# Attention loop: softmax division in place in PSUM, output projection in three rounded passes, mask product in one pass, side jobs in other rounds

## The reference, cut to what matters

```python
q = (x @ Wq).reshape(b, s, 16, 64)          # b = 1, s = 2048, x is [2048, 128]
k = (x @ Wk).reshape(b, s, 16, 64)
v = (x @ Wv).reshape(b, s, 16, 64)
dot = jnp.einsum('bihd,bkhd->bhik', q, k)
w = jax.nn.softmax(dot / jnp.sqrt(64.), axis=-1)
a = jnp.einsum('bhij,bjhd->bihd', w, v).reshape(b, s, 1024)
out = a @ Wo + bo
```

## Time and profile before

| | us |
|---|---|
| median of 3 runs (1913.63 to 1916.16) | 1915.83 |
| the profiled execution | 1917.79 |
| its span, first to last instruction | 1916.5 |
| TensorE busy | 1685.4 (88%) |
| VectorE busy | 1327.3 (69%) |
| GpSimd busy | 1286.8 (67%) |
| ScalarE busy | 787.4 (41%) |
| 32 maximum-and-score units, about 443 to 1739 | some 1300 |

### The profile page before, as it was taken

The page is one execution under the profiler, slowest core; times in us unless marked ns, Lnnn a source line. Parts: engine busy times, 40 slices in busy tenths (PEclk is TensorE's granted clock), DMA queues, the critical chain, the costliest instruction groups (busy, mean ns, idle before and its releaser), DMA issues.

```text
span 1916.5 us, 34532 instructions
## 1 busy us (share of the span) xinstructions
PE 1685.4 (88%) x13785; PEld 986.1 (51%) x13785; DVE 1327.3 (69%) x2083; ACT 787.4 (41%) x1183; POOL 1286.8 (67%) x652
## 2 busy tenths in 40 slices
PE   4988851848999999999999999999999999995793
PEld 3766641825555555555555555555555545442483
DVE  3566545666777777777777777777777788764575
ACT  3455430523444444444444444444444444442221
POOL 2233303135988888888888888888888889894303
PEclk8677755969999999999999999999999999997797
DMA  7000000210000000000000000000000000002112
GB/s 237 3 3 3 4 1 20 62 28 1 1 1 1 1 1 1 1 1 1 1 1 1 1 1 1 1 1 1 1 1 1 1 1 1 1 1 81 49 42 61
DMA packets 35190, 29.70 MB, mean 15 GB/s; under 512 B 4060, under 2 KB 30928, under 8 KB 35032
## 3 DMA queue, kind: packets, MB, share of 16 engines
q1 hardware_dynamic: 27064, 20.28, 3.5%
q0 software_dynamic: 2048, 4.20, 0.7%
q10 hardware_dynamic: 5920, 3.01, 0.5%
HBM read 18.31 MB, written 9.18 MB: 14 GB/s over the span
## 4 chain that ended last, share of the span: by engine, by line
PE 68%; DVE 8%; issue 6%; POOL 3%; DMA 1%; ACT 1%; DVEq 0%; POOLq 0%
PE psum L1799 22%; PE psum L1784 16%; PE psum L1759 9%; PE psum L1781 6%; DVE a_On L1994 3%; DVE a_mx L1962 3%; PE psum L1431 2%; PE psum L1813 2%; PE psum L1807 2%; PE psum L1732 1%; PE psum L1392 1%; PE psum L1207 1%; PE psum L1219 1%; PE psum L1441 1%; PE psum L1733 1%
## 5 line engine op out<-in xcount | busy, mean ns | idle before, releaser
L2075 POOL TENSOR_TENSOR a_acc<-a_acc,a_Pb 128x1024 f32<-128x1024 f32 x448 | 1066.0, 2379 | 147.0 <-ACT a_Pb L1899 102.0
L1962 DVE TENSOR_REDUCE a_mx<-psum 128x2 f32<-128x1024 f32 x512 | 624.9, 1223 | 274.7 <-PE psum L1759 274.2
L1899 ACT ACTIVATE a_Pb<-psum 128x1024 f32<-128x1024 f32 x512 | 498.1, 1024 | 646.5 <-PE psum L1784 646.5
L1799 PE MATMUL psum<-a_Pb,a_Vb 128*64 128x512 f32 x2048 | 494.1, 603 | 0.0
L1799 PEld LDWEIGHTS psum<-a_Pb,a_Vb 128*64 128x64 f32 x2048 | 127.0, 136 | 242.5 <-issue 171.8
L1759 PE MATMUL psum<-a_Kh,a_Qh 64*128 64x512 f32 x1024 | 237.3, 457 | 15.5 <-DVE a_mx L1962 15.0
L1759 PEld LDWEIGHTS psum<-a_Kh,a_Qh 64*128 64x128 f32 x1024 | 99.2, 184 | 251.9 <-issue 243.2
L1781 PE MATMUL psum<-a_Mr,a_ones_r 64*128 64x512 f32 x1024 | 203.8, 393 | 0.0
L1784 PE MATMUL psum<-a_Qh,a_Kh 64*128 64x512 f32 x1024 | 202.9, 391 | 0.0
L1784 PE MATMUL psum<-a_Ql,a_Kh 64*128 64x512 f32 x1024 | 202.8, 391 | 0.0
L1784 PE MATMUL psum<-a_Qh,a_Kl 64*128 64x512 f32 x1024 | 202.3, 389 | 0.0
(11 more groups left out here) (372 smaller groups left out, 1905.1 us busy)
## 6 DMA issues: line engine op xcount, KB each, us to landing
x_rows<-zero ACTq DMA_DIRECT2D x2, 1472.0 KB, 15.7
g_w<-in_L_ffn_w_eDF_dram SPq DMA_DIRECT2D x2, 1408.0 KB, 8.8
r_W<-in_L_ffn_W_dram SPq DMA_DIRECT2D x1, 2048.0 KB, 11.5
r_tile_x<-x_rows SPq DMA_DIRECT2D x23, 64.0 KB, 1.9
y_rows<-r_tile_y SPq DMA_DIRECT2D x23, 64.0 KB, 1.5
g_tile_x<-x_rows SPq DMA_DIRECT2D x23, 64.0 KB, 1.9
y_rows<-g_tile_y SPq DMA_DIRECT2D x23, 64.0 KB, 1.5
g_w<-in_L_ffn_w_eFD_dram SPq DMA_DIRECT2D x2, 512.0 KB, 10.8
```

Of the source, the lines that this page charges most:

```text
L1799: last = pe.matmul(ps[HEAD[h], B_O, :], b.Vb[:, p // 2 % 2, kc, at], b.Pb[:, step % BUFS, h * QT:(h + 1) * QT], start=(kc == 0), stop=(kc ...
L1899: act.activation(b.Pb[:, step % BUFS, :], ps[:, slot:slot + 2, :].rearrange("p a b -> p (a b)"), ACT.Exp, scale=SCALE).then_inc(S["probs"], 1)
L1962: v.tensor_reduce(b.mx[:, :, qc, quarter:quarter + 1], ps[:, bank:bank + 2, :], AX.X, ALU.max).then_inc(S[f"free{bank}"], 1)
L2075: g.tensor_tensor(b.acc[:, u, :], before, b.Pb[:, step % BUFS, :], ALU.add).then_inc(S["added"], 1)
```

## The change

What it does:

- The sums stay in bank 7. VectorE inverts them there, in four parts of 128 columns, two in round 2 and two in round 3. It multiplies them by `Or` in one instruction of 512 columns, in the same bank, at the end of round 3.
- ScalarE copies the result, rounded, into `Onh`; VectorE subtracts this in round 4 into `Onl`, which frees bank 7. `ssum`, `rec` and `On` go.
- `Wo` is split into a high and a low part at the start, as the three other weights are, and the output projection becomes three rounded passes, in round 5 of the next unit.
- `mask` multiplies two float32r operands; a rounded identity is made for it.
- `out` moves from round 2 (for unit U - 2) to round 5 (for unit U - 1), `v` from round 3 to round 6.

```diff
@@ misc_job
-    if d == 2 and U > 1:
-        return "out", U - 2
...
+    if d == 5 and U:
+        return "out", U - 1
...
@@ attention_weights_act, attention_weights_pool: four matrices where there were three
-    k.nc.scalar.wait_ge(k.S["att_w"], 48)
-    for m in range(3):
-        k.nc.scalar.activation(k.att_w[m][0][:, :], k.att_raw[:, m, :], ACT.Copy).then_inc(k.S["w_high"], 1)
+    k.nc.scalar.wait_ge(k.S["att_w"], 64)
+    for m, (hi, _) in enumerate((*k.att_w, k.att_o)):
+        k.nc.scalar.activation(hi[:, :], k.att_raw[:, m, :], ACT.Copy).then_inc(k.S["w_high"], 1)
...
@@ attention_pe
     def mask(U):
+        if U == 0:
+            pe.wait_ge(S["ident_r"], 1)
         pe.wait_ge(S["negated"], U + 1)
         bank = begin(("mask", U))
-        end(pe.matmul(ps[:, bank, 0:P], b.nm[:, :], k.ident[:, :], start=True, stop=True), bank)
+        end(pe.matmul(ps[:, bank, 0:P], b.nm[:, :], b.ident[:, :], start=True, stop=True), bank)
...
     def output(U):
-        pe.wait_ge(S["normalised"], 4 * U + 4)
+        freed(("sum", U))
         bank = begin(("out", U))
-        end(pe.matmul(ps[:, bank, :], k.att_o[:, U // NU, :], b.On[:, :], start=True, stop=True), bank)
+        hi, lo = (w[:, U // NU * P:(U // NU + 1) * P] for w in k.att_o)
+        pe.matmul(ps[:, bank, :], hi, b.Onh[:, :], start=True, stop=False)
+        pe.matmul(ps[:, bank, :], lo, b.Onh[:, :], start=False, stop=False)
+        end(pe.matmul(ps[:, bank, :], hi, b.Onl[:, :], start=False, stop=True), bank)
@@ attention_act
-    def sums(U):
-        bank = begin(("sum", U))
+    def normalised(U):
+        act.wait_ge(S["normalised"], U + 1)
         if U:
-            act.wait_ge(S["inverted"], 4 * U)
-        act.activation(b.ssum[:, :], ps[:, bank, :], ACT.Copy).then_inc(S[f"free{bank}"], 1)
+            bank, n = plan.at["out", U - 1]
+            act.wait_ge(S[f"full{bank}"], n)
+        act.activation(b.Onh[:, :], ps[:, plan.at["sum", U][0], :], ACT.Copy).then_inc(S["high_out"], 1)
...
-        if key and key[0] == "sum":
-            sums(U - 1)
         if d == 0 and U:
             heads_out(U - 1)
+        if d == 3 and U:
+            normalised(U - 1)
@@ attention_dve
     def invert(U, part):
-        if U and part == 0:
-            v.wait_ge(S["normalised"], 4 * U)
-        bank, n = plan.at["sum", U]
-        v.wait_ge(S[f"free{bank}"], n)
+        bank = begin(("sum", U))
         at = slice(part * P, (part + 1) * P)
-        v.reciprocal(b.rec[:, at], b.ssum[:, at]).then_inc(S["inverted"], 1)
+        v.reciprocal(ps[:, bank, at], ps[:, bank, at]).then_inc(S["inverted"], 1)
+
+    def normalise(U):
+        v.wait_ge(S["inverted"], 4 * U + 4)
+        v.wait_ge(S["heads_out"], U + 1)
+        bank = plan.at["sum", U][0]
+        v.tensor_tensor(ps[:, bank, :], ps[:, bank, :], b.Or[:, U % 2, :], ALU.mult).then_inc(S["normalised"], 1)
+
+    def normalised_low(U):
+        bank = plan.at["sum", U][0]
+        v.wait_ge(S["high_out"], U + 1)
+        if U:
+            last_out, n = plan.at["out", U - 1]
+            v.wait_ge(S[f"full{last_out}"], n)
+        v.tensor_tensor(b.Onl[:, :], ps[:, bank, :], b.Onh[:, :].bitcast(F32), ALU.subtract).then_inc(S[f"free{bank}"], 1)
...
-        if U and 2 <= d <= 5:
-            invert(U - 1, d - 2)
+        if U and d in (2, 3):
+            for part in (2 * d - 4, 2 * d - 3):
+                invert(U - 1, part)
+        if U and d == 4:
+            normalised_low(U - 1)
...
-        if U and d in (3, 5, 6, 7):
-            normalise(U - 1, (3, 5, 6, 7).index(d))
+        if U and d == 3:
+            normalise(U - 1)
```

More of the change, by code:

```diff
@@ L1594, in misc_job @@
         return "sum", U - 1
-    if d == 2 and U > 1:
-        return "out", U - 2
-    if d == 3 and p // 2 < PAIRS // 2 - 1:
-        return "v", p // 2 + 1, U % RN
     if d == 4 and U < UNITS - 2:
         return "q", U + 2
+    if d == 5 and U:
+        return "out", U - 1
+    if d == 6 and p // 2 < PAIRS // 2 - 1:
+        return "v", p // 2 + 1, U % RN
     if d == 7 and U < UNITS - 1:
@@ L1638, in __init__ @@
                 self.job(misc_job(R), B_P)
-        for key in (("out", UNITS - 2), ("sum", UNITS - 1), ("out", UNITS - 1)):
+        for key in (("sum", UNITS - 1), ("out", UNITS - 1)):
             self.job(key, B_P)
@@ L1656, in allocate_attention_weights @@
     k.att_w = [[k.sb(f"att_W{a}{part}", [P, PAIRS * P], F32R) for part in "hl"] for a in "qkv"]
-    k.att_o, k.att_b = k.sb("att_Wo", [P, PAIRS, P]), k.sb("att_b", [P, 1])
+    k.att_o = [k.sb(f"att_Wo{part}", [P, PAIRS * P], F32R) for part in "hl"]
+    k.att_b = k.sb("att_b", [P, 1])
 def allocate_attention_raw(k, mem):
-    k.att_raw = k.sb("att_raw", [P, 3, PAIRS * P], F32, mem)
+    k.att_raw = k.sb("att_raw", [P, 4, PAIRS * P], F32, mem)
 def allocate_attention(k, mem):
@@ L1676, in allocate_attention @@
     b.Or = sb("Or", [P, 2, QT])
-    b.On = sb("On", [P, QT])
-    b.ssum = sb("ssum", [P, QT])
-    b.rec = sb("rec", [P, QT])
+    b.Onh, b.Onl = (sb(a, [P, QT], F32R) for a in ("Onh", "Onl"))
     b.mx = sb("mx", [P, 2, 4, NU])
-    b.nm = sb("nm", [P, P])
+    b.nm = sb("nm", [P, P], F32R)
+    b.ident = sb("ident_r", [P, P], F32R)
     b.plan = Plan()
@@ L1688, in attention_loads_sp @@
         sp.dma_start(k.att_raw[:, m, :], io[name]).then_inc(S["att_w"], 16)
-    sp.dma_start(k.att_o[:, :, :], io["L1_attn_Wo"].rearrange("(a p) d -> p a d", p=P)).then_inc(S["att_wo"], 16)
+    sp.dma_start(k.att_raw[:, 3, :].rearrange("p (a d) -> p a d", a=PAIRS), io["L1_attn_Wo"].rearrange("(a p) d -> p a d", p=P)).then_inc(S["att_w"], 16)
 def attention_weights_act(k):
-    k.nc.scalar.wait_ge(k.S["att_w"], 48)
-    for m in range(3):
-        k.nc.scalar.activation(k.att_w[m][0][:, :], k.att_raw[:, m, :], ACT.Copy).then_inc(k.S["w_high"], 1)
+    k.nc.scalar.wait_ge(k.S["att_w"], 64)
+    for m, (hi, _) in enumerate((*k.att_w, k.att_o)):
+        k.nc.scalar.activation(hi[:, :], k.att_raw[:, m, :], ACT.Copy).then_inc(k.S["w_high"], 1)
 def attention_weights_pool(k):
     S, g = k.S, k.nc.gpsimd
-    for m in range(3):
+    for m, (hi, lo) in enumerate((*k.att_w, k.att_o)):
         g.wait_ge(S["w_high"], m + 1)
@@ L1703, in attention_weights_pool @@
             g.wait_ge(S["w_low"], m)
-        hi, lo = k.att_w[m]
         g.tensor_tensor(lo[:, :], k.att_raw[:, m, :], hi[:, :].bitcast(F32), ALU.subtract).then_inc(S["w_low"], 1)
@@ L1825, in attention_pe @@
         end(last, bank)
-    pe.wait_ge(S["w_low"], 3)
+    pe.wait_ge(S["w_low"], 4)
     freed(("x", 0))
@@ L1842, in attention_pe @@
     pe.wait_ge(S["att_ready"], 1)
-    pe.wait_ge(S["att_wo"], 16)
     for R in range(ROUNDS):
@@ L1855, in attention_pe @@
     weigh(ROUNDS - 1)
-    output(UNITS - 2)
     sums(UNITS - 1)
@@ L1903, in heads_out @@
         if U > 1:
-            act.wait_ge(S["normalised"], 4 * U - 4)
+            act.wait_ge(S["normalised"], U - 1)
         act.activation(b.Or[:, U % 2, :], ps[:, B_O, :], ACT.Copy).then_inc(S["heads_out"], 1)
@@ L1908, in attention_act @@
     act.activation(b.ones[:, :], k.ones[:, :], ACT.Copy)
+    act.activation(b.ident[:, :], k.ident[:, :], ACT.Copy).then_inc(S["ident_r"], 1)
     gather_norm_act(k, 1)
@@ L1925, in attention_act @@
             {"q": queries, "k": keys, "v": values}[key[0]](*key[1:])
-        if key and key[0] == "sum":
-            sums(U - 1)
         if d == 0 and U:
             heads_out(U - 1)
+        if d == 3 and U:
+            normalised(U - 1)
     heads_out(UNITS - 1)
-    sums(UNITS - 1)
+    normalised(UNITS - 1)
     for g in range(4):
@@ L1979, in invert @@
     def invert(U, part):
-        if U and part == 0:
-            v.wait_ge(S["normalised"], 4 * U)
-        bank, n = plan.at["sum", U]
-        v.wait_ge(S[f"free{bank}"], n)
+        bank = begin(("sum", U))
         at = slice(part * P, (part + 1) * P)
-        v.reciprocal(b.rec[:, at], b.ssum[:, at]).then_inc(S["inverted"], 1)
-    def normalise(U, part):
-        v.wait_ge(S["inverted"], 4 * U + part + 1)
+        v.reciprocal(ps[:, bank, at], ps[:, bank, at]).then_inc(S["inverted"], 1)
+    def normalise(U):
+        v.wait_ge(S["inverted"], 4 * U + 4)
         v.wait_ge(S["heads_out"], U + 1)
[L1990 to L1994, removed]
+        bank = plan.at["sum", U][0]
[7 more added lines that the diff above has]
+        v.tensor_tensor(b.Onl[:, :], ps[:, bank, :], b.Onh[:, :].bitcast(F32), ALU.subtract).then_inc(S[f"free{bank}"], 1)
     def output(U):
@@ L2005, in attention_dve @@
     v.memset(b.mask[:, :, :], 0.0)
-    dve.did(v.memset(b.nm[:, :], 0.0))
+    dve.did(v.tensor_scalar(b.nm[:, :], k.ident[:, :], 0.0, None, ALU.mult))
     dve.wait()
@@ L2041, in attention_dve @@
             {"q": queries, "k": keys, "mask": mask, "out": output}[key[0]](*key[1:])
-        if U and d in (3, 5, 6, 7):
-            normalise(U - 1, (3, 5, 6, 7).index(d))
-    output(UNITS - 2)
+        if U and d == 3:
+            normalise(U - 1)
     for part in range(4):
```

(3 more changed lines are left out.)

## The result

The changed kernel took 1892.92 us (median of 4 runs, 1886.38 to 1894.25) against 1915.99 before: a ratio of 0.9874 to 0.9878 in two measurements, the first with a 95% interval of 0.9856 to 0.9901. That is 23 us, 1.2%, faster. The forecast was 1911.6, a gain of 4 us, with 1903 as the lower end of its range. The direction held; the size did not.

The account below looks back on a forecast made before the run. TensorE was taken to set the pace (busy 1286 of 1310 us). Some 36 us taken away against 32 us of new waits gave 4.2 gained: 1917.8 - 4.2 = 1913.6, less 1.96, 1911.6 us; range 1903 to 1922.5.

Parts of the forecast that it names:

- The four `a_On` go, and the waits of rounds 7 and 0 with them: VectorE's four normalising pieces a unit vanish, and TensorE's waits of 0.63 in round 7 and 0.26 in round 0.
- Rounds 2 and 3 at 4.90: Two reciprocals between late and early maximum stretch each round to 4.90 us (4.81 to 4.97), against 4.36 bare.
- The 0.09 for the restart: Rounds 2 and 3: array runs empty during the wait; about 0.1 added, half certain, taking 4.81 to 4.90.
- The mask at half its saving: Round 7: one rounded pass of 128 columns saves between 0 and 0.15; half taken, giving 4.72.
- The wait for bank 7 in round 4: TensorE wants the bank for q at 2.49 but can have it at 2.53: a wait of 0.04.
- Output 1.07 to 0.89: Output projection, moved to round 5, becomes three passes like q: 0.89 us for 1.07.
- The end: Behind the last addition: 9.5 us after the change against 9.7 before, 0.2 gained.
- Unit 30, up to the sums of the last unit: Round 0 gains 0.3; GpSimd, busy from round 2 on, makes that round 5.02, not 5.43: 0.4 gained.
- Start of the kernel, free: One more ScalarE copy and GpSimd subtraction, before idle times of 57.4 and 45.5 us, cost nothing.
- cheaper waits: Rival: no restart cost and full mask saving take 7 us off, at most 12; middle 1903, chance 0.17.
- Dearer reciprocals in PSUM: Rival: each reciprocal in rounds 2 and 3 costs 0.065 more, 7.8 us back, 1919.4; chance 0.14.
- Collision: Rival: reading and writing one bank slows reciprocals in rounds 2 and 3; at 0.1 each 12 us, 1923.6; chance 0.17.

Follow-up runs that it names:

- narrow additions: The kernel before the change, with GpSimd's additions cut from 1024 to 64 columns (sums then hold one in the rest); one run, 1881.0 us.

## Why the prediction was wrong, step by step

- *TensorE sets the pace, inside the unit*: right. All that moved the time moved a wait or a length in TensorE's queue.
- *The four `a_On` go, and the waits of rounds 7 and 0 with them, 0.63 and 0.26*: right, 0.57 and 0.24 by the run with narrow additions. Their cause was not known at the time: the 2.00 was read from the row as if it were the instruction's own length; alone it takes 0.28.
- *Rounds 2 and 3 at 4.90*: this is the step that failed. The mechanism was right, the new wait between two maxima; its size was not. It set what a round loses at 0.54, and it is 0.28 (4.66 against a bare round of 4.38). In parts: the 1.75 of two reciprocals counts the second to its end, though the next instruction starts 0.08 before that (the 1.14 put for the maximum in front of them did take in such an overlap); the early maximum was put at 1.23 and takes 1.16 in that place (0.07); and 0.09 was added for restarting the array, which costs nothing there. Together 0.24 a round, 60 rounds, 14.4 us.
- *The 0.09 for the restart* is worth a closer look, because such a cost exists elsewhere. A late product is followed by scores, which have the same shape in the array; they start 0.31 behind it where it had waited (58 cases between 500 and 1650 us) and 0.34 where it had not (173). An early product is followed by another shape. There the next product starts 0.43 behind it where it had waited, in the kernel before (973.49 to 973.92, the mask of round 7), and 0.34 where it had not (narrow additions). So the waits of before cost more than their hand-over, as the prediction noted, and those of rounds 2 and 3 do not.
- *The mask at half its saving*: 4.72 put, 4.62 measured, 3 us. The saving was the whole of the 0.15 that was given as its upper end, and a little more.
- *The wait for bank 7 in round 4*: 0.04 put, none seen (the query product stands 0.32 behind the early one, as everywhere), 1 us.
- *Output 1.07 to 0.89*: right within 0.02. *The end* 9.5 put, 9.3 measured.
- *Unit 30, up to the sums of the last unit*: 0.7 gained by the forecast, 0.76 by the profiles (from the gathering of unit 30 to the sums 83.56 before, 82.80 after).
- *Start of the kernel, free*: not shown. The attention starts at the same time within 0.5 us in the two profiles, but this start scatters by 12 us from run to run.

The three wrong sizes add to 0.48 + 0.10 + 0.03 = 0.61 of the 0.63 by which a middle unit was off (40.80 put, 40.17 measured). Over 29 units that is 18 of the 19 us by which the forecast missed. And the gain itself, by the runs, in a middle unit: 0.81 of old waits gone, 0.16 less in the output, 0.22 less in the mask, 0.56 of new waits. That makes 0.63, where 0.68 was measured.

Of the rivals, "cheaper waits" points the right way: no restart cost and the mask at its full saving were both real, 7 us. It is not what happened in full. Its far end was 12 us under the forecast, 1899.6, by 0.04 less in each reciprocal, and no run shows that reciprocals in PSUM are shorter (0.955, against 0.943 in SBUF before). The overlap and the shorter maximum, 0.15 a round and 9 us, stood in no rival. "Dearer reciprocals in PSUM", the rival from the table of the Trainium skill, did not happen: 0.955 against 0.951. The formula that the prediction set against that table is the page's for a sum of two tensors, not for a product; products of 512 columns here lie near it too (0.699 in the earlier trace rows, 0.691 to 0.692 for `t_dg` of line 696). "Collision" did not happen either: that same 0.955, in place in one bank.

Of the signs named beforehand, the period of a middle unit, 40.17, lies outside 40.5 to 41.2, so by its own test the forecast was wrong. The waits came 60 times, as said, but at 0.22 and not at half a microsecond. The mask adds 0.24 to a bare round, less than the 0.29 to 0.44 given. Rounds 2 and 3 at 4.66 stayed inside their 4.6 to 5.1. The forecast was a difference of two sums, 36 us taken and 32 given, so that a small error in a count of 4.81 weighed heavily: 0.26 less in each of 60 rounds turned 32 into 17.

## What to carry to other kernels

Where one buffer goes back and forth between two engines, count the room between its uses, and put side work where there is room; two short instructions in one gap cost what one in each of two gaps does not. In such a count, use the distance from start to start, not the durations. And when an instruction's duration scatters from 0.23 to 2.45 us, look at what ends with it on the other engines before calling it slow.

## What the runs showed of the hardware

- A VectorE instruction that reads two fp32 tensors from SBUF, or a scaled fp32 copy, stands still while a GpSimd addition of 2.37 us runs, and ends 0.02 us (2 columns) to 0.15 us (128 columns) after it, the scaled copy 0.08: in 120 to 122 of 128 cases. A product with one operand in PSUM takes 0.68 for 512 columns beside the same additions.
- A reciprocal of 128 columns takes 0.94 to 0.96 if it is the first of a row and 0.90 behind another, whether its source is in SBUF or in PSUM, and with source and target in the same bank. The maximum behind it starts 0.81 after the start of the second of two.
- A maximum of 1024 columns that waited for its data takes 1.23, one whose data lay ready 1.16 behind two reciprocals and 1.21 behind a product that GpSimd had held up.
- A TensorE product of another shape starts 0.43 to 0.50 us behind a maximum product that had waited, and 0.32 to 0.34 behind one that had not; one of the same shape 0.31 and 0.34.
- A float32r pass of 128 columns between products of another shape costs 0.26 in the chain, an fp32 one in two records 0.42.
